# A stage's loads, constants and bias tables moved beside the norm ahead of it, and a butterfly table computed inside attention

## The reference

```python
def layer(x):                        # four times, with other attentions and ffns
    xn = layernorm(x)
    s = attention(xn, ...)
    g = silu(ffn(xn, ...))
    return x + s * g
# layer 0, ffn: 9 butterfly stages turn W_exp, b_exp and W_con^T into the dense matrices used,
#   (y0, y1) -> (w00*y0 + w01*y1, w10*y0 + w11*y1) for all pairs; then gelu(xn @ up + b) @ down + b
# layer 2, attention: bias[h, i, j] = cumsum(rpe_bias)[h, i - j] for i >= j, else -30000
# layer 3, attention: two Mamba scans, forward and reversed
```

## Time and profile before

| | us |
|---|---|
| median of 3 runs (lowest, highest) | 4221.18 (4212.93, 4227.74) |
| the profiled execution, its own time | 4199.25 |
| its span | 4197.5 |
| busy: PE, PEld, DVE, ACT, POOL | 3475.4, 2290.4, 2421.9, 1864.2, 1741.1 |
| HBM read, written | 233.21 MB, 54.53 MB |

### The profile page before, as it was taken

How to read it: one execution, slowest core, us unless ns; L and a number is a source line. 1 busy time by engine, 2 the same in 40 slices (tenths; PEclk the granted TensorE clock), 3 DMA queues, 4 the chain that set the end, 5 groups by cost and what they waited for, 6 DMA issues and landing times. The chain is left out here.

```text
span 4197.5 us, 71439 instructions
## 1 busy us (share of the span) xinstructions
PE 3475.4 (83%) x24836; PEld 2290.4 (55%) x24836; DVE 2421.9 (58%) x5353; ACT 1864.2 (44%) x5088; POOL 1741.1 (41%) x1926
## 2 busy tenths in 40 slices
PE   5888826673999997999999799977999999995581
PEld 2565612351666664666665344434777777774460
DVE  2666672451666664666665344444888888894233
ACT  4666612451666663545444100035666666651120
POOL 3545541320666663333332000014666666672406
PEclk7999967885999998999999999998999999996795
DMA  3777730004000000000000676732222222223122
GB/s 105 204 190 199 196 100 15 10 1 80 1 1 1 1 1 12 2 2 1 1 2 20 143 152 152 152 71 72 72 78 75 76 76 74 73 81 106 57 70 63
DMA packets 268012, 292.36 MB, mean 70 GB/s; under 512 B 60745, under 2 KB 179466, under 8 KB 267403
## 3 DMA queue, kind: packets, MB, share of 16 engines
q1 hardware_dynamic: 260970, 274.16, 25.4%
q0 software_dynamic: 4096, 8.40, 0.6%
q10 hardware_dynamic: 2592, 5.26, 0.3%
HBM read 233.21 MB, written 54.53 MB: 69 GB/s over the span
## 5 line engine op out<-in xcount | busy, mean ns | idle before, releaser
L2260 DVE TENSOR_TENSOR_SCAN a_h<-a_dA,a_dBu_psum 128x512 f32<-128x512 f32 x512 | 595.7, 1204 | 165.1 <-issue 103.7
L1193 POOL TENSOR_SCALAR a_probs<-a_probs,a_row_inv 128x128 f32<-128x128 f32 (+1 forms) x512 | 381.3, 762 | 278.4 <-DVE a_row_inv L1179 278.4
L2217 POOL TENSOR_TENSOR a_h<-a_h,main_g 128x512 f32<-128x512 f32 x256 | 384.0, 1502 | 271.4 <-DVE a_h L2260 261.4
L1984 PE MATMUL a_dBu_psum<-a_B_diag,a_dt_u_turned 64*128 64x128 f32 x4096 | 316.9, 289 | 21.5 <-DVE a_h L2260 20.7
L1726 DVE SCALAR_TENSOR_TENSOR m_hidden<-m_h_psum,m_gate_spread 128x512 f32<-128x512 f32 x256 | 176.7, 691 | 263.7 <-PE m_h_psum L1664 249.4
L1518 POOL TENSOR_TENSOR r_position_q<-r_turned_q 128x512 f32<-128x512 f32 x128 | 159.6, 1269 | 389.2 <-DVE r_turned_q L1563 389.2
L190 POOL TENSOR_TENSOR main_g<-main_g,main_s 128x512 f32<-128x512 f32 x28 | 43.9, 1600 | 643.9 <-ACT main_g L173 643.9
L1984 PEld LDWEIGHTS a_dBu_psum<-a_B_diag,a_dt_u_turned 64*128 64x128 f32 x4096 | 257.8, 188 | 76.1 <-issue 71.2
L1475 ACT ACTIVATE r_probs<-r_logits_psum,r_neg_max 128x256 f32<-128x256 f32 x512 | 235.5, 476 | 140.3 <-DVE r_neg_max L1569 140.3
L2005 PE MATMUL a_y_psum<-main_ident,a_h 128*128 128x128 f32 x2048 | 275.2, 276 | 7.7 <-POOL a_h L2217 6.7
L1671 PE MATMUL m_o_psum<-m_hidden,f_values 128*128 128x512 f32 x512 | 262.4, 595 | 8.6 <-DVE m_hidden L1726 8.6
(11 more groups left out here) (534 smaller groups left out, 7759.4 us busy)
## 6 DMA issues: line engine op xcount, KB each, us to landing
m_gate_spread<-m_gate_rows SPq DMA_DIRECT2D x64, 1024.0 KB, 8.2
main_g<-a_b_c_rows SPq DMA_DIRECT2D x256, 256.0 KB, 3.2
a_band_rows<-main_g SPq DMA_DIRECT2D x64, 512.0 KB, 3.5
a_B<-a_band_rows SPq DMA_DIRECT2D x192, 128.0 KB, 3.2
a_A<-a_band_rows SPq DMA_DIRECT2D x192, 128.0 KB, 3.0
f_x_rows<-f_zero ACTq DMA_DIRECT2D x16, 320.0 KB, 9.0
f_x_expert<-f_x_rows SPq DMA_DIRECT2D x16, 320.0 KB, 2.8
f_y_rows<-f_y_expert SPq DMA_DIRECT2D x16, 320.0 KB, 2.2
```

What stands on the lines that cost most here:

```text
L1193: ins = nc.gpsimd.tensor_scalar(pr[:, h % NPR, tile[t]], pr[:, h % NPR, tile[t]], rinv[:, p % NST, q:q + 1], None, ALU.mult)
L1984: ins = mm(dst[:, :, tc * P + HALF * half:tc * P + HALF * (half + 1)], dtuT[U % 2][rows, q, tc, k * P:(k + 1) * P], diag[rows, M % NDIAG, ...
L2217: tt(h[:, r, :, :], h[:, r, :, :], Cs[:, g % NCS, :, :], ALU.mult).then_inc(hc_pool, 1)
L2260: nc.vector.tensor_tensor_scan(flat, dA[:, M % NDA, q, k, :, :].rearrange("p n t -> p (n t)"), db[:, 2 * (g % 2) + k, :], 0.0, ALU.mult, A ...
```

## The change

- `load` and its blocks go. `gate_and_norm` gets an argument `beside`: functions for SP, POOL, ACT and three places on DVE (`vector_first` ahead of the gating, `vector_between` behind it, `vector_last` at the end), with semaphores of their own. The norm in front of a stage is now called inside the stage, behind its tile allocations. POOL's function waits for all products first.
- Layer 0: the set-up comes first and loads x as the last of its DMAs; the fills of v and A move from POOL to DVE. The first norm loads the FFN's weights and the weights of the first two butterfly halves beside it. The 18 halves (162 TENSOR_TENSORs, the bias row among them) run on DVE in attention, three in each iteration; SP loads each further half's weights (512 KB) between band writes. W_con comes transposed from the host's layout, so its first transposition goes.
- FFN of layer 0: one block with transposes and all eight chunks; no hardware loop.
- Layer 1: 25 loads beside the norm (`ahead`), POOL's constants too.
- Layer 2: all loads of its attention and of its FFN's tables, the sums (`vector_first`), the bias write and its reads beside the norm. The sums are written 32 times over instead of 128 times (768 KB instead of 3 MB), and read back in eight pieces of 32 partitions instead of two of 128. The constants of `relative_attention` too.
- Layer 3: 18 loads, folding (`vector_between`), exp of A (at ACT's end), its negation and POOL's constants beside the norm.

```diff
@@ gate_and_norm
+        def also(place, engine):
+            if beside and place in beside:
+                beside[place](engine, *own)
...
             @block.vector
+                also("vector_first", dve)
                 if gate:
                     for k in range(N):
                         if not on_pool(k):
                             product(k)
                         add(k)
+                also("vector_between", dve)
...
             @block.sync
                 for dst, src in loads:
                     sp.dma_start(dst, src, allow_slow_non_contiguous=True).then_inc(landed, 16)
                 for dst, src in ahead:
                     sp.dma_start(dst, src, allow_slow_non_contiguous=True).then_inc(ahead_in, 16)
+                also("sync", sp)
@@ l0_attention, set-up
-                    nc.gpsimd.memset(v[:], 0.0)
                     nc.gpsimd.memset(B[:], 0.0)
-                    nc.gpsimd.memset(A[:], 0.0)
...
                         sp.dma_start(w[:], d[n]).then_inc(rest_in, 16)
+                    sp.dma_start(x[:], x_home).then_inc(x_in, 16)
                     sp.wait_ge(rest_in, 16 * 14)
+                    sp.wait_ge(x_in, 16)
...
+                    nc.vector.memset(v[:], 0.0)
+                    nc.vector.memset(A[:], 0.0)
                     dve.wait_ge(mm, 1)
...
             t.barrier()
+        gate_and_norm(nc, c, x, xn, ahead=tables.loads() + [tables.weights(0), tables.weights(1)])
@@ l0_attention, DVE
+                def turn_table():
+                    n, op = next(ops, (None, None))
+                    if op is None:
+                        return
+                    h = op[0]
+                    if h >= 2 and n == tables.first_of(h):
+                        dve.wait_ge(weight_in[h % 2], 16 * (h // 2))
+                    if n:
+                        dve.wait_ge(turned_op, n)
+                    tables.turn(nc.vector, op).then_inc(turned_op, 1)
...
+                    if p < NQ:
+                        turn_table()
+                        turn_table()
                     if band_of(p) is not None:
                         keep_band(band_of(p))
+                    if p < NQ:
+                        turn_table()
@@ l0_attention, SP
+                def put_weights(h):
+                    sp.wait_ge(turned_op, tables.first_of(h - 1))
+                    dst, src = tables.weights(h)
+                    sp.dma_start(dst, src).then_inc(weight_in[h % 2], 16)
...
+                def write_and_load(n):
+                    write(n)
+                    while due[0] is not None and (tables.first_of(due[0] - 1) - 1) // 3 <= n - 6:
+                        put_weights(due[0])
+                        due[0] = next(halves, None)
@@ l0_ffn
-        with nc.Fori(0, xn.shape[1] // (W * PER) or 1) as i:
...
+                pe.wait_ge(made, 1)
+                for f in range(NF):
+                    nc.tensor.matmul(tp[:, 1, f:f + 1], upb[:, f * P:(f + 1) * P], one[:], start=True,
+                                     stop=True).then_inc(biased, 1)
+                for f in range(NF):
+                    nc.tensor.transpose(tp[:, 0, f * P:(f + 1) * P], dn[:, f * P:(f + 1) * P], c["ident"][:]).then_inc(turned, 1)
+                raise_(0)
+                pe.wait_ge(kept, 2)
+                for k in range(NCH):
+                    if k + 1 < NCH:
+                        raise_(k + 1)
+                    lower(k)
@@ l2_attention
+            def sums(dve, rpe_in, zeroed, padded, summed, ready, *_):
+                nc.vector.memset(zero[:], 0.0).then_inc(zeroed, 1)
+                nc.vector.memset(rev[:], PAD / SC).then_inc(padded, 1)
+                dve.wait_ge(rpe_in, 16)
...
+                nc.vector.tensor_scalar(rev[:, 0:T], cum[:, ::-1], 1.0 / SC, None, ALU.mult).then_inc(ready, 1)
+
+            def spread(sp, rpe_in, zeroed, padded, summed, ready, rows_out, bias_in, *_):
+                sp.dma_start(rb[:], d["rpe_bias"]).then_inc(rpe_in, 16)
+                sp.wait_ge(ready, 1)
+                sp.dma_start(rows, rev[:].unsqueeze(1).broadcast_to([H, R, T + P])).then_inc(rows_out, 16)
+                sp.wait_ge(rows_out, 16)
+
+                for tile in range(2):
+                    for q in range(0, P, R):
...
+                        sp.dma_start(bias[q:q + R, :, P * tile:P * (2 * tile + 1)], src).then_inc(bias_in, 16)
+            gate_and_norm(nc, c, x, xn, s_out, g, gate=True, again=(g, vec[:, 0:1], vec[:, 1:2]), loads=loads, ahead=ahead,
+                          beside={"sems": "rpe_in zeroed padded summed ready rows_out bias_in " + beside["sems"],
+                                  "vector_first": sums, "sync": spread, "pool": beside["pool"],
+                                  "vector_last": beside["vector_last"]})
@@ l3_attention
+        gate_and_norm(nc, c, x_res, xn, s_out, spare, gate=True, again=(normed, vec[:, 0:1], vec[:, 1:2]),
+                      loads=[(vec[:, i:i + 1], column(d[v])) for i, v in enumerate(("ln_g", "ln_b"))],
+                      beside={"sems": "weights_in A_exp flip_zero", "sync": load_weights, "vector_between": fold_conv,
+                              "scalar": exp_A, "vector_last": negate_A, "pool": constants})
```

More of the change, by code:

```diff
@@ L99, in make_constants, with gate_and_norm @@
     return c
-def load(nc, scope, pairs):
-    with Scope(nc, scope.name + "_load") as s:
-        landed = s.sems("landed")
-        with nc.Block() as block:
-            @block.sync
-            def _(sp):
-                for dst, src in pairs:
-                    sp.dma_start(dst, src, allow_slow_non_contiguous=True).then_inc(landed, 16)
-                sp.wait_ge(landed, 16 * len(pairs))
-        s.barrier()
 def column(v):
     return v.rearrange("(c p) -> p c", p=min(P, v.shape[0]))
-def gate_and_norm(nc, c, x, xn, s=None, g=None, gate=False, norm=True, out=None, affine=None, again=None, loads=(), ahead=()):
+def gate_and_norm(nc, c, x, xn, s=None, g=None, gate=False, norm=True, out=None, affine=None, again=None, loads=(), ahead=(), beside=None):
     W = BANK
@@ L190, in _ @@
                             nc.gpsimd.tensor_tensor(g[:, cols(k)], g[:, cols(k)], s[:, cols(k)], ALU.mult).then_inc(mixed_pool, 1)
+                    if beside:
+                        pool.wait_ge(mixed_pool, before(N - 1))
+                also("pool", pool)
             @block.vector
@@ L949, in l2_attention @@
+        s.barrier()
+def l2_attention(nc, c, d, vec, loads, ahead, beside, x, xn, s_out, g):
     HD = 64
@@ L1279, in relative_attention @@
+        (wq, wk, wv, wo, wpos), rot, key_trig, pick, mask, v = tables
         qs, qm, kc = s.sb("q", [P, T]), s.sb("q_masked", [P, 2, NG, T]), s.sb("k", [P, 2, T])
@@ new lines, in fold_conv, with exp_A @@
+        def fold_conv(dve, weights_in, *_):
+            dve.wait_ge(weights_in, 16 * len(pairs))
+            for w, dd in zip(W, D_diag):
+                for i in range(KC):
+                    nc.vector.tensor_tensor(w["conv"][:, i, :], w["conv"][:, i, :], w["in"][:, 0:DI], ALU.mult)
+                for k in range(NK):
+                    nc.vector.tensor_scalar(dd[:, k, :], c["ident"][:], w["D"][:, k:k + 1], None, ALU.mult)
+        def exp_A(act, weights_in, A_exp, *_):
+            act.wait_ge(weights_in, 16 * len(pairs))
+            for w in W:
+                nc.scalar.activation(w["A"][:], w["A"][:], ACT.Exp).then_inc(A_exp, 1)
@@ new lines, in negate_A, with constants @@
+        def negate_A(dve, weights_in, A_exp, *_):
+            dve.wait_ge(A_exp, 2)
+            for w in W:
+                nc.vector.tensor_scalar(w["A"][:], w["A"][:], -1.0, None, ALU.mult)
+        def constants(pool, weights_in, A_exp, flip_zero):
+            nc.gpsimd.memset(flip[:], 0.0).then_inc(flip_zero, 1)
+            for i in range(NDA):
+                nc.gpsimd.memset(dA[:, i, :, :, :, 0:1], 0.0)
+            pool.wait_ge(flip_zero, 1)
+            nc.gpsimd.affine_select(out=flip[:], in_=flip[:], compare_op=ALU.not_equal, fill=1.0, base=1 - P,
+                                    pattern=[[1, P]], channel_multiplier=1)
@@ new lines, in third_layer @@
+def third_layer(nc, c, da, d, x, xn, s, g):
+    E = 32
+    with Scope(nc, "f2") as f:
+        vec = f.sb("vectors", [P, 4])
+        tables, ahead, beside = relative_tables(f, d)
+        l2_attention(nc, c, da, vec, [(vec[:, i:i + 1], column(d[n])) for i, n in enumerate(("ln1_g", "ln1_b", "ln2_g", "ln2_b"))],
+                     ahead, beside, x, xn, s, g)
+        relative_attention(nc, c, tables, xn, g, g)
+        x2 = f.sb("normed", [P, xn.shape[1]])
+        weights = keys, vals, selw = f.sb("keys", [P, E, P]), f.sb("values", [P, E, P]), f.sb("sel_w", [P, E])
+        gate_and_norm(nc, c, g, x2, affine=(vec[:, 2:3], vec[:, 3:4]),
+                      ahead=[(selw[:], d["sel_w"]), (keys[:], d["keys"].rearrange("e p n -> p e n")),
+                             (vals[:], d["values"].rearrange("e p n -> p e n"))])
```

(1 more changed line is left out.)

517 lines of the change are left out of this document (203 added, 314 removed).

## The result

| | before | after |
|---|---|---|
| median of 4 runs each (lowest, highest), us | 4221.57 (4212.93, 4227.74) | 4014.94 (4011.69, 4020.06) |
| ratio | | 0.9513, 95% interval 0.9493 to 0.9533 |
| profiled execution, its span, us | 4199.25, 4197.5 | 4015.36, 4013.6 |
| busy: PE, DVE, ACT, POOL | 3475.4, 2421.9, 1864.2, 1741.1 | 3466.1, 2415.3, 1855.5, 1704.5 |

What follows compares the result with a forecast made beforehand. Set-ups running alone between all-engine barriers cost their whole length, with no engine at 100% in the first attention. 215.4 us won less 42 gives 173 net: profiled 4199.25 becomes 4026, or 4048 against the median, range 4000 to 4100.

Steps and rivals of the forecast that it cites:

- rival A: Layer 0's attention: POOL's masks don't meet the table operations, 6 us given back instead of 42; 4012 us, chance 0.22.
- Head: Start to first projection: set-up goes first, x loads behind its DMAs and ends last, first projection at 47.3; -11.4 us.
- done at 10.9: Head's set-up: DVE's fills of v and A, priced by POOL's 2.2 + 5.2 us, end at 10.9.
- Butterfly and FFN set-up: Between layer 0's attention and hidden matmul, barrier and transposes stay, -103.6 us; FFN as one run, -11.9 us.
- Attention: Layer 0: 162 TENSOR_TENSORs in DVE's gaps, two of four gaps costing, 3.0 to 3.1 us a group, +42 us.
- Term (i): Attention, gap before the late mask: POOL is held up for all three table operations, +1.6 us.
- Term (ii): Attention, next gap: products slowed by POOL's masking and the third operation ahead of the inversion, +1.4 us.
- the lower end: Attention: only the third operation costs, 0.45 us once in four iterations, 13.5 x 0.45 = 6 us.
- Third layer: Loads, sums, bias write and reads move beside the norm, whose additions wait for `rpe`; -38.9 us.
- B: Rival, layer 0's attention: every gap costs what the late-mask gap does, 6.5 us a group, +88; 4094 us, chance 0.16.
- C: Rival, layer 0's attention: DVE and POOL hold each other up in every iteration, 247 us; 4253 us, chance 0.02.
- D: Rival, third layer: norm and eight reads don't overlap as put, only half the win comes; 4068 us, chance 0.13.

Runs made afterwards that it cites:

- e9: Changed kernel with `rpe` loaded first, table operations 2, 4, 4, 0 a phase, v and A filled ahead of DVE's first norm: 4000.71 us, ratio 0.9466.
- e2: Changed kernel without the 162 table operations in attention and SP's 16 weight DMAs: ratio 0.9474 to the kernel before, attention 497.8 us.
- e3: Changed kernel with all table operations but only the first two halves' weights loaded: ratio 0.9502 to the kernel before, attention 509.1 us.
- e7: Changed kernel with the 162 table operations placed 2, 4, 5 and 0 to the four phases: ratio 0.95 to the kernel before, attention 510.5 us.
- e4: Changed kernel with the load of `rpe` issued first beside the norm before layer 2: ratio 0.9467 to the kernel before.
- e1: The kernel before, unchanged, run once more: median 4232.36 us, ratio 1.0 to the kernel before beside it.
- e8: Changed kernel with each table operation replaced by a TENSOR_SCALAR with one SBUF operand: ratio 0.9516 to the kernel before, attention 510.7 us.
- e6: Changed kernel with `rpe` loaded first and the row write next, ahead of the 23 other loads before layer 2: ratio 0.9495 to the kernel before.

## Why the prediction was right, and by how much it was off

It said 4048 us with 4000 to 4100, and 4014.9 was measured: inside, 33 below the likeliest value. Of the 33, 27 are the attention, whose price was put too high by a factor of 2.8, and 5.5 the stages that the change doesn't touch. The time isn't within 15 us of 4048, which had 0.45; it lies at rival A's 4012, which had 0.22. That it came so near to 4012 is luck, since A's mechanism isn't what the runs show.

- **Head.** -9.1 instead of -11.4. The step "done at 10.9" failed: DVE's fill of A ended at 12.58, because DVE began 0.6 us into the block and stood 1.23 us between its two fills. It stands 1.23 us between them in e9 too, where POOL's fill is long over, so that is no blocking by POOL's fill of B. The set-up, not x, ended last, at 19.34 instead of 18.6, which the prediction had named as a sign of being wrong, and the norm begins at 20.3 instead of 19.2. That is 1.1 us; the rest is in the norm behind it, since the first projection comes at 46.0 to 48.8 in the kernels with this head, with the same start at 20.3. That the TENSOR_SCALAR of 4.86 us was POOL's fill of A is borne out: 0.32.
- **Butterfly and FFN set-up.** Right, 3.0 us from attention to the hidden matmul instead of 4.7, since the raise doesn't wait for the transposes' copy. The FFN in one block: -12.1 for -11.9. Its cold start was put at 0.9 us beside rows of 9.7 and 7.1, which are 2.6 apart, so the reading doesn't give the term; measured, the first raise takes 8.20, 1.1 over the warm one.
- **Attention.** The places were right: one of four gaps ahead of the late mask, one ahead of the inversion, the other two free, and weights that nobody waits for (e2, e3, e7). The sizes were wrong: this is the step that failed. Term (i) was 1.6 us a group, the whole length of the three operations, and measured 0.69. The rows of the butterfly were the wrong price for it: there both engines ran TENSOR_TENSORs against each other, and here POOL reads one operand. The masks do meet the tables, contrary to rival A, but of 1.8 us of DVE work some 0.6 come through: four head masks 0.48 longer, a pair of band masks 0.17. DVE's products suffer little: their medians are 0.60 to 0.63, with 0.60 alone, though single ones take up to 0.94; the sums of `f_up` have a median of 0.62, with 0.42 alone. Term (ii) was 1.4 and measured 0.39 to 0.41, close to the 0.45 of the lower end, because it holds the third operation alone, the products costing 1.25 and not 2.05. There too it is POOL that gives way (a pair of band masks takes 1.36 and not 1.00 beside the products), and nobody waits for those masks. 0.69 + 0.39 = 1.08 a group, by 13.5 it is 14.6, where the ledger has 14.8.
- **Second layer.** Right, -16.1 for -16.8.
- **Third layer.** Right to 0.7 us and by its own steps: DVE's wait for `rpe` was put at about 18 us and was 19.71, the additions at 21.5 behind the norm's start and measured at 21.5, the reads under the norm. The prediction named this wait as the price of the change's order, and e4 shows that 11 us of it can be had back and that the reads hold the rest: they land 5.8 us after DVE's last operation of the norm. In the changed kernel itself they land at 833.9, 5 us ahead of the norm's end, as forecast.
- **Relative tables and fourth layer.** -16.6 for -16.5, -16.4 for -16.3. Folding ran in DVE's pause.
- **Median against profile.** The prediction set the difference against the median, 21.9 above the profiled execution. e1 shows why that was the right side: the profiled one lacked 26 us in a stage that costs them in every other profile.

Rival A's time (4012) was the nearest, but not its mechanism: POOL's masks were held up, and 14.8 us were given back instead of 6; most of that difference is made up by the 5.5 us of stages that the change doesn't touch. B would have needed every gap to cost what the late one does: phases 1 and 2 are unchanged to 0.01 us. C needed 4.0 us an iteration and got 0.26. D fell: the third layer's overlap gave 38.2.

## What to carry to other kernels

A set-up in a block of its own between two barriers costs its whole length, and moving it beside a norm gives that length back almost to the microsecond; what needs working out is the one operation in it that waits for the last DMA of a long queue while the norm stands behind it. Work that is put into an engine's gaps should be placed phase by phase: here one gap took four operations for nothing (phase 1, 0.04 us longer in e7), one took three (a fourth cost 0.24 in phase 2), one took two, and the larger part of the cost came from the one gap in which another engine was already late. Take the price of two engines meeting from rows with the same kinds of operands on both sides; what was inferred here from rows of another pair was 2.3 times too high for that gap (1.6 us, measured 0.69).

## What the runs showed of the hardware

- DVE's form decides whether POOL is held up. POOL's 128x256 TENSOR_SCALAR takes 0.555 us alone and beside TENSOR_REDUCEs of DVE, 0.671 in the mean (0.895 at most) beside TENSOR_TENSORs with two SBUF operands, 0.636 beside one-operand TENSOR_SCALARs of 128x512.
- The hold-up is partial here: about 0.6 us of POOL for 1.8 us of DVE in the late gap. It falls mostly on POOL, but not only: a DVE TENSOR_SCALAR of 128x512 went from 0.41 to 0.88 us beside POOL's masks (e8), and a sum from 0.42 to 0.62 in the median.
- In the kernel before it looks whole: DVE's TENSOR_SCALAR of 128x64 beside POOL's fill of A took 4.86 us and ended at 53.68, 0.05 us behind the fill; it takes 0.32 without one.
- Behind a DMA of 768 KB in 512 rows of 1.5 KB two issues of SP took 4.12 and 3.04 us instead of 0.43 (e6). That the number of pieces is the reason isn't shown.
- While POOL issued 64 scattering DMAs, ACT and DVE started 10 to 18 us behind what they waited for in the profile of after, and the stage was as long in eleven profiles of twelve. The cause is open, and no run here was made for it.
